# Pairing the value products of a causal attention kernel on TensorE, in a list schedule that is recomputed for it

## The reference, cut to what matters

```
xn  = layernorm(x)                                # x: 2 x 2048 x 256
q   = rope(xn @ wq)   # 16 heads of 16            k = rope(xn @ wk), v = xn @ wv   # 4 key/value heads of 16
s   = q k^T / 4, causal mask over 2048 keys       # each k/v head serves 4 q heads
out = softmax(s) v, heads joined, @ wo
y   = real(ifft(fft(xn) @ w)) + bias              # a fixed 256 x 256 matrix, made on the chip
result = x + out + y
```

## Time and profile before

| | |
|---|---|
| median of 3 runs | 1010.68 us (1005.64 to 1014.27) |
| the profiled execution | 1008.69 us, span 1006.9 us |
| TensorE busy | 961.0 us (95% of the span) |
| VectorE busy | 737.4 us (73%) |
| ScalarE busy | 650.7 us (65%) |
| GpSimd busy | 325.1 us (32%) |
| mean granted TensorE clock | 0.956 |

### The profile page before, as it was taken

One profiled execution on the slowest core, in us unless ns is written; L12 is line 12 of the kernel. 1 busy time (PEld: TensorE's weight loads), 2 busy tenths in 40 slices (PEclk: granted clock), 3 DMA queues, 4 the chain that ended last, 5 costly groups with the idle time before them and its releaser, 6 DMA issues.

```text
span 1006.9 us, 17764 instructions
## 1 busy us (share of the span) xinstructions
PE 961.0 (95%) x6792; PEld 471.1 (47%) x6792; DVE 737.4 (73%) x894; ACT 650.7 (65%) x1303; POOL 325.1 (32%) x350
## 2 busy tenths in 40 slices
PE   8989899999999989999999999999999999999998
PEld 6644455445444434443354554544444444544424
DVE  7686677767787787777888776677878887788801
ACT  2433566664676655676777666676767766677785
POOL 6287683868136300133500132327210100100000
PEclk9867699999999996999999999999999997999989
DMA  5645005152211210010200311001510000000000
GB/s 162 138 136 107 23 32 106 44 109 70 67 35 48 58 13 17 12 48 2 68 17 6 64 44 49 12 11 34 95 34 11 2 1 1 12 12 1 1 1 22
DMA packets 37701, 43.50 MB, mean 43 GB/s; under 512 B 11376, under 2 KB 23280, under 8 KB 37616
## 3 DMA queue, kind: packets, MB, share of 16 engines
q1 hardware_dynamic: 37616, 42.36, 17.2%
HBM read 27.13 MB, written 14.68 MB: 42 GB/s over the span
## 4 chain that ended last, share of the span: by engine, by line
PE 84%; ACT 8%; DVE 5%; issue 2%; DMA 0%; SPq 0%; POOL 0%; ACTq 0%
PE psO L1357 28%; PE psA L1293 20%; PE psS L1340 18%; ACT prob_sb L975 6%; PE psS L1266 4%; PE psS L1325 3%; PE psS L1327 2%; DVE pmax L1102 2%; PE psA L1298 2%; DVE pmax L1104 2%; PE psS L1273 1%; PE psA L1308 1%; ACT oraw_sb L984 1%; PE psS L1317 1%; PE psA L1365 1%
## 5 line engine op out<-in xcount | busy, mean ns | idle before, releaser
L975 ACT ACTIVATE prob_sb<-psS 128x512 f32<-128x512 f32 (+2 forms) x1108 | 560.0, 586 | 226.3 <-PE psS L1340 223.6
L1104 DVE TENSOR_REDUCE pmax<-psA 128x2 f32<-128x1024 f32 x384 | 459.9, 1220 | 116.9 <-PE psA L1293 115.7
L1340 PE MATMUL psS<-q_st,k_st 50*128 50x512 f32 (+3 forms) x1232 | 397.9, 432 | 5.2 <-ACT prob_sb L975 4.3
L1293 PE MATMUL psA<-k_st,q_st 48*128 48x512 f32 (+3 forms) x1280 | 360.7, 428 | 15.6 <-DVE pmax L1104 7.0
L1357 PE MATMUL psO<-prob_sb,v_sb 128*17 128x512 f32 (+3 forms) x2560 | 305.8, 551 | 15.5 <-ACT prob_sb L975 7.7
L1293 PEld LDWEIGHTS psA<-k_st,q_st 48*128 48x128 f32 x1280 | 177.9, 193 | 249.1 <-DVE pmax L1104 90.0
L1102 DVE TENSOR_REDUCE pmax<-psA 128x4 f32<-128x512 f32 (+2 forms) x192 | 198.7, 1046 | 87.0 <-PE psA L1298 85.9
L859 POOL TENSOR_SCALAR_AFFINE_SELECT prob_sb<-prob_sb 128x512 f32<-128x512 f32 x128 | 81.1, 635 | 499.2 <-ACT prob_sb L975 487.2
L1340 PEld LDWEIGHTS psS<-q_st,k_st 50*128 50x128 f32 x1232 | 195.0, 192 | 93.7 <-ACT prob_sb L975 83.4
L1357 PEld LDWEIGHTS psO<-prob_sb,v_sb 128*17 128x17 f32 x2560 | 43.2, 96 | 104.4 <-issue 40.9
L1298 PE MATMUL psA<-mask_r,mask_l 64*128 64x64 bf16 (+1 forms) x768 | 80.3, 213 | 0.0
(11 more groups left out here) (106 smaller groups left out, 570.3 us busy)
## 6 DMA issues: line engine op xcount, KB each, us to landing
q_st<-parts_scratch SPq DMA_DIRECT2D x174, 64.0 KB, 2.5
parts_scratch<-parts SPq DMA_DIRECT2D x64, 128.0 KB
k_st<-parts_scratch SPq DMA_DIRECT2D x48, 128.0 KB, 4.4
q_st<-spartT SPq DMA_DIRECT2D x256, 2.0 KB
x_sb<-in_L_attn_x SPq DMA_DIRECT2D x7, 512.0 KB, 4.1
out<-x_sb SPq DMA_DIRECT2D x14, 256.0 KB, 2.3
parts_scratch<-parts SPq DMA_DIRECT2D x32, 64.0 KB
oraw_sb<-in_L_attn_x SPq DMA_DIRECT2D x1, 1536.0 KB, 11.7
```

The lines of the kernel that those rows point to most:

```text
L975: nc.scalar.activation(prob[:, g % DEEP, r0:r0 + hp, s0:CH], bank_at(bank)[:, 0:hp * w].rearrange("p (h s) -> p h s", h=hp), ACT.Exp).then ...
L1104: nc.vector.reduce_max(pmax[:, heads[0]:heads[0] + 3:2, i, q], psA[:, two:two + 2, :], AX.X).then_inc(S["a_free"], 1)
L1293: last = mm(bank[:, k * w:(k + 1) * w], q_st[lo:lo + ROWS, n % (2 * KV), heads[o * per + k] % 2, i * P:(i + 1) * P], k_st[lo:lo + ROWS, sl ...
L1340: last = mm(bank[:, h * w:(h + 1) * w], k_st[lo:lo + FULL, key_slot(n, tile), kv, tile % CT * P:(tile % CT + 1) * P], q_st[lo:lo + FULL, n ...
```

## The change

`v_ready` gets one more condition: the values of an even unit may be taken only when the exponentials (or, on the diagonal, the mask) of the odd unit after it are planned too. A rule ahead of the others takes the odd unit's values straight after the even one's. The bias addition of a chunk rises in GpSimd's queue (rank 0.6 instead of 2.5) once its first `e3` product is planned. Where nothing is ready, the planner moves its clock on by 0.5 us instead of stopping. No instruction is added or taken out and no buffer is changed: DEEP stays 3 and RING stays 3. Only the orders differ.

```diff
@@ v_ready
             at = exp_at[g]
             if UNITS[n][u][3] is not None:
                 at = mask_at.get(g, big)
+            if g % 2 == 0:
+                at = max(at, (exp_at if UNITS[n][u + 1][3] is None else mask_at).get(g + 1, big))
             if u == 0 and n > 0:
                 at = max(at, copied[n - 1] if len(copied) >= n else big)
@@ do_back
                 e3_at[cc, h, job[3]] = end
+                for k, e in enumerate(pool_jobs):
+                    if e[3] == ("bias", cc):
+                        pool_jobs[k] = (e[0], 0.6) + e[2:]
                 add_pool(act + 0.1, 0.7, ("add", cc, h, job[3]))
@@ the choice of the next job
             elif aside and pe and pe[-1][0] == "pv" and now - aside_at > 2.5 and act - now > 0.5:
                 choice = aside
+            elif ready["v"] <= soon and next_v % 2 == 1 and pe[-1] == ("pv", next_v - 1):
+                choice = "v"
             elif ready["a"] <= soon and dve - now < 1.4:
                 choice = "a"
...
             else:
                 first = min(ready.values())
-                assert first < big, (ready, next_b, next_v, next_a, stage[:1], back[:1])
+                if first >= big:
+                    now += 0.5
+                    assert now < 5000.0, (ready, next_b, next_v, next_a, stage[:1], back[:1])
+                    continue
```

## The result

The changed kernel is slower: 1060.91 us (median of 4 runs, 1056.6 to 1064.04) against 1009.62 us before, a ratio of 1.049 with a 95% interval of 1.044 to 1.054. I had forecast 1015, with 1040 as the upper end.

A forecast was written before the change was run, and what follows sets the result against it. TensorE and VectorE were taken to share the bound where j = 3, TensorE to be late elsewhere. + 13 - 11 + 4 = + 6 us on the profiled 1008.69 gave 1015, range 995 to 1040.

The forecast's parts named there:

- Fewer changes from full to split work: On TensorE, values directly behind values save 0.12 us; 139 stretches fewer, 17 us less where TensorE sets the pace.
- Longer stretches: Merged split work waits longer for VectorE in steps with j = 3: 0.135 us per full unit, 13 us.
- there I let a merge lengthen nothing: Outside j = 3, TensorE is late for its partners anyway, so 91 merges gain 11 us.
- What paces them: In long split stretches VectorE's reductions, one every 1.13 us, set the pace; ScalarE paces the scores too, but less.
- The start: First values wait for unit 1's exponentials and mask, behind unit 2's scores and a slot of maxima: 4 us at worst.
- The clock: Half-clock stretches anywhere: one of 17 us more or less moves the end by up to 8 us.
- The slower rival: VectorE's pace holds in every full unit, not only at j = 3: + 25 us, 1034; chance 30%.

The follow-up runs named there:

- both partners light: Reductions and exponentials over half the columns each, in the changed kernel and the one before: 932.4 us changed, 944.8 us before.
- pairs_jlow: The changed kernel with pairs only in the steps with j = 0, 1 and 2: 1030.34 us, ratio 1.020 to the kernel before.
- light kernels: Both kernels with half-column reductions, exponentials, or both: before 1000.0, 967.6, 944.8 us; changed 1035.0, 1018.5, 932.4 us.
- no_pairs: The changed kernel with the v_ready condition and the odd unit's rule switched off: 1011.88 us, ratio 1.002 to the kernel before.

## Why the prediction was wrong

By its steps, in sums over all stretches from start to start, from the first values on:

- **Fewer changes from full to split work: right.** A pair of values lasts 1.84 us. All stretches of full work together should have become 17 us shorter. With both partners light they did by 12 (410.2 to 398.5). As the kernels are, they became 17 us longer (413.8 to 430.5): stretches of values alone lie 39.7 us over their own full-clock lengths in the changed kernel, and 10.8 before. That is + 29 at the half clock, which more than eats the gain. Taken at full-clock lengths, the stretches of values alone did become 17 us shorter.
- **Longer stretches: the lengths right, the places wrong.** 2.72 for six and six and 3.81 for eight and eight (3.66 for those wholly at full clock) are near the forecast's 2.72 and 3.80. The first step that failed is "there I let a merge lengthen nothing". Split work became 33 us longer in all, 10.5 at j = 3 and 22 in the other steps. A line fitted to the kernel before's stretches at full clock (time by the counts of maxima and scores) gives 25 us of this for the changed mix of lengths. That is about 0.2 us for each of 139 merges, more than the 0.12 a merge saves. I had booked some 19 (13, with the saving for 48 merges taken out of it) at j = 3, which was too much, and nothing elsewhere, which was too little. About 6 more lie in stretches at half clock. pairs_jlow shows a loss where I had a gain. My reason, that VectorE has time there, looked at one partner over 100 us. A stretch is paced in its own 3 us, by two slots and three banks, however idle the partners are on average.
- **What paces them: half right.** I named VectorE and waved ScalarE off. The light kernels show both, each enough by itself.
- **The start: the number by luck.** The first values began at 73.9 instead of 69.8, 4.1 us for 4. But they began at 73.9 in the trace of no_pairs too, whose orders are those of the kernel before. What the change did is seen from the first score to the first values: 3.95 us in both traces of the old order, 9.48 in the changed kernel. Unit 1's exponentials and mask, which I had named, were not in the way: they were done by 71.1. The slot of maxima that now stands ahead of the values waited for VectorE, which had the layernorm's statistics ahead of its reductions:

```profile
73.10 0.69 PE L1303 MATMUL psA<-k_st,q_st 48*128 48x384 f32 x2 [3.71 <-DVE pmax L1112]
```

- **The clock: this is the large miss**, and the second step that failed. "It belongs to no rival, and widens the range", by 8 us. I took its falls as weather, and they go with long stretches in which TensorE waits: 28 against 4, and 6 in the same order with both partners light. 74 us more were spent at half clock, at a cost of + 29 in the values and about 11 in all else, by the sums here. Without these 40 us the same sum would be + 12, for the + 6 forecast.

The parts: - 17 (fewer changes) + 29 and + 5 (values and other full work, mostly at half clock) + 25 and + 6 to 8 (split work) + 4 (start, which isn't told from scatter) = 52 to 54, and the span grew by 53.3. The sizes of the clock's parts are read from the trace. No run took the clock away by itself, so its share is argued and not shown. That the loss needs the partners' pace is shown: with both light it is gone, and the clock is near that of the kernel before with the same edit. The slower rival had the right mechanism, every stretch paced. Its price was wrong in two ways: 25 to 33 us for the waits, where the sum without the clock gives 12, and nothing for the clock.

I had the rows for it. After its first values the kernel before drops to half clock at 103, 376, 830 and 967. The first three falls lie in stretches of split work of 7.9, 12.6 and 6.3 us, the last directly behind one of 3.3. I read only when, not behind what. The Trainium skill (TensorEngine Tiling (Array Packing), Performance Considerations) warns that tiling does not speed up the emptying of PSUM. The traces agree: with the work of both engines that empty it made light, eight and eight went from 3.81 to 2.94 us.

## What to carry to other kernels

Price a reordering by what stands between the moved pieces, not only by the saved changeover. If an engine works through a few buffers that others empty, short alternation hides their latency. Merging two fillings can then cost more than the switch it saves, as here (about 0.2 us against 0.12), even with the others idle a quarter of the time. And where a profile has granted clocks, look what stood ahead of each fall before treating it as chance.

## What the runs showed of the hardware that I had not expected

- TensorE, 95% busy by its row, fell to the lower of its two clock levels 28 times after the first values, mostly in or behind stretches that the list of waits hardly knows.
- Of two consumers of nearly equal pace (1.13 us for a reduction, 1.02 for two exponentials), relieving one hardly helped: with reductions cut from 1.22 to 0.69 us, a stretch of eight and eight went from 3.81 to 3.71, with exponentials cut from 0.59 to 0.37 to 3.62, with both to 2.94.
- 34 groups of four full-row matmuls, an estimated 19 us of work (0.55 us each), made no difference to the time of the kernel before beyond 0.4% (ratio 1.000, 0.996 to 1.004), on an engine that its profile calls 95% busy.
